# Weaving the routing, the metric of batch 0 and the first chunks into the projection loop of an adaLN block, with the layer normalisation moved from VectorE to GpSimd

## The reference, cut to what matters

```python
mod = (silu(c) @ wmod).reshape(8, 6, 1, 128)      # sa, ca, ga, sb, cb, gb
h = layernorm(x) * (1 + ca) + sa
x = x + ga' * attn(h)                              # ga', gb': sign(g) * max(|g|, 0.25)
h = layernorm(x) * (1 + cb) + sb
x = x + gb' * ffn(h)

# attn, 8 heads of 16, for each token t a causal window of 64 tokens
q, v = relu(h @ enc_q), relu(h @ enc_v)
sig  = q.mean(tokens) + 0.5 * q[::8].mean(tokens)              # one vector per batch
m    = softplus(base + 0.1 * (gelu(sig @ w1 + b1) @ w2 + b2))  # "metric", per batch
dist = sqrt(((q[window] - q[t])**2 * m).sum() + 1e-8)
keep the 32 nearest of the 64; w = exp(-dist) / sum
context = sum(w * v) + gate * 0.1 * (q / |q|) @ (U @ V)        # "Hebbian" term
attn = (q * context) @ decoder

# ffn: 8 experts of rank 64, mixed with gates that depend on token 0 of each batch
logits = h[:, 0] @ Wr.T ; gates = softmax over the two largest logits
ffn = h + sum_e gates[e] * (h @ A[e].T) @ B[e].T
```

## Time and profile before

| | us |
|---|---|
| three runs | 840.10, 841.48, 842.94 |
| the profiled execution | 845.14 |
| its span in the trace | 843.4 |
| first MAX8 of the first chunk | 91.19 |
| start of the fifth step of DVE (i = 4) | 140.29 |
| busy: DVE, PE, ACT, POOL | 788.9 (94% of the span), 718.6 (85%), 619.5 (73%), 463.0 (55%) |

### The profile page before, as it was taken

The page is one execution under the profiler, slowest core; times in us unless marked ns, Lnnn a source line. Parts: engine busy times, 40 slices in busy tenths (PEclk is TensorE's granted clock), DMA queues, the critical chain, the costliest instruction groups (busy, mean ns, idle before and its releaser), DMA issues.

```text
span 843.4 us, 21229 instructions
## 1 busy us (share of the span) xinstructions
PE 718.6 (85%) x4437; PEld 586.2 (70%) x4437; DVE 788.9 (94%) x6746; ACT 619.5 (73%) x1862; POOL 463.0 (55%) x871
## 2 busy tenths in 40 slices
PE   5997989888888888888888888888888888888845
PEld 3445677777777777777777777777777777777744
DVE  5855999999999999999999999999999999999980
ACT  3981368787777878777777877777878777787853
POOL 2112456666556566655656665565566655656541
PEclk9996989999999999999999999999999999999955
DMA  5310001101111110011110001111100111111000
GB/s 165 102 32 10 24 24 30 30 20 32 31 31 31 29 30 24 27 31 30 32 30 29 26 24 32 31 31 30 30 29 21 31 31 31 31 30 30 18 4 9
DMA packets 49232, 27.24 MB, mean 32 GB/s; under 512 B 5512, under 2 KB 48592, under 8 KB 49104
## 3 DMA queue, kind: packets, MB, share of 16 engines
q1 hardware_dynamic: 49104, 25.90, 10.4%
HBM read 10.28 MB, written 4.19 MB: 17 GB/s over the span
## 4 chain that ended last, share of the span: by engine, by line
DVE 83%; PE 10%; DMA 2%; ACT 2%; issue 2%; POOL 1%; SPq 1%; ACTq 0%; POOLq 0%
DVE work L976 44%; DVE m L965 29%; DVE key L998 4%; DMA big<-in_x 2%; DVE st_c L1007 1%; PE psD L1152 1%; DVE mv_c L1019 1%; PE psC L1182 1%; DVE key L787 1%; PE psD L1057 1%; DVE st_p L778 1%; PE psC L1085 1%; PE psW L1239 1%; DMA wmod_sb<-in_wmod 1%; PE psW L1168 1%
## 5 line engine op out<-in xcount | busy, mean ns | idle before, releaser
L976 DVE MATCH_REPLACE8 work<-m,work 128x64 f32<-128x64 f32 x1536 | 301.8, 208 | 0.0
L1152 PE MATMUL psD<-sst,tst 128*128 128x224 f32 x1024 | 238.9, 356 | 0.0
L965 DVE MAX8 m<-work 128x8 f32<-128x64 f32 x1536 | 209.9, 209 | 0.0
L1152 PEld LDWEIGHTS psD<-sst,tst 128*128 128x128 f32 x1024 | 196.3, 192 | 3.2 <-issue 0.3
L452 POOL TENSOR_TENSOR big<-work,con 128x512 f32<-128x512 f32 x128 | 162.2, 1291 | 13.0 <-ACT work L635 12.9
L481 POOL TENSOR_TENSOR t<-cst,qh 128x128 f32<-128x128 f32 x64 | 27.8, 434 | 232.3 <-ACT cst L714 232.3
L1182 PE MATMUL psC<-vst,big 128*128 128x34 f32 x1024 | 129.0, 272 | 0.0
L1182 PEld LDWEIGHTS psC<-vst,big 128*128 128x128 f32 x1024 | 128.4, 197 | 0.2
L976 DVE MATCH_VALUE_LOAD work<-m,work 128x8 f32 x1536 | 120.0, 78 | 0.0
L976 DVE MATCH_REPLACE8 work<-m,key 128x64 f32<-128x64 f32 x512 | 100.2, 208 | 0.0
L1149 PE MATMUL psD<-mask_bf,ident_bf 128*128 128x448 bf16 x256 | 91.1, 356 | 9.3 <-DMA tst<-nst 1.8
(11 more groups left out here) (199 smaller groups left out, 1474.7 us busy)
## 6 DMA issues: line engine op xcount, KB each, us to landing
hst<-hT_all SPq DMA_DIRECT2D x64, 96.0 KB
tst<-qT_all SPq DMA_DIRECT2D x256, 17.0 KB
big<-in_x SPq DMA_DIRECT2D x16, 256.0 KB, 2.8
tst<-nst SPq DMA_DIRECT2D x256, 1.0 KB
xs<-in_x SPq DMA_DIRECT2D x64, 64.0 KB, 1.9
out<-yo SPq DMA_DIRECT2D x64, 64.0 KB, 1.7
sst<-nst SPq DMA_DIRECT2D x128, 3.0 KB
con<-in_consts SPq DMA_DIRECT2D x1, 549.5 KB, 5.8
```

What stands on the lines that cost most here:

```text
L965: last = v.max(m8[:, h], src[:, h * WIN:(h + 1) * WIN])
L976: last = v.match_replace(work[:, s, cols], m8[:, h], src[:, cols], GONE)
L1152: last = mm(bank_of(r)[:, g, 0:SW], tst[:, s, r, g], sst[:, s, g], start=False, stop=(g == NG - 1), skip_group_check=True)
```

## The change: what it does

1. **Normalisation on POOL.** DVE only makes `nb = -mean * rstd` (one small instruction per unit, `nbias`), POOL does `x * rstd + nb` in four tensor_scalar instructions per unit. On ACT Ln and Exp of a unit now stand next to each other, between `to_hT(n+1)` and `to_q(n)`.
2. **Token 0 by itself.** Mean, variance, modulation and q of the eight first tokens are made ahead of unit 0 from `x0_sb` (`t0T`, `q0T`), so that the routing doesn't wait for the projection.
3. **`unit_extra(n)`.** On ACT, DVE and PE each unit n ends with a piece of the routing chain, of the metric of batch 0 (`METRIC[0]`), of the norms and values of chunks 0 and 1 (n = 10 to 13) and of the gate rows (n = 12 to 14).
4. **The other seven metrics** (`METRIC[1]`) run in steps 0 to 3 of the top-k: Gelu and its two table loads on ACT at i = 0, softplus on ACT at i = 1 and on POOL at i = 2 and 3, one reciprocal on DVE.
5. **Gate x B** is made wholly on POOL, in two halves of four 128x512 instructions; `experts(0)` is on PE at i = 0, `experts(1)` inside step 1, `expert_matrices(0)` on DVE inside step 0 and (1) ahead of step 2.
6. **Start of the pipeline.** `FIRST` is -1 instead of -3; the distances of chunk 0 follow the last unit on PE.
7. **Loads** are issued in another order; the constants are split so that the identity comes early; modn goes through psD instead of psW.

The core of the diff (SP's reordered issues, the pieces of `unit_extra` that only move, and the helper functions made of old lines are left out):

```diff
@@ POOL
+            def normalise(n):
+                u = n % 4
+                pool.wait_ge(nb_ready, n + 1)
+                need(pool, pT_ready, n - 1)
+                for c in range(4):
+                    last = nc.gpsimd.tensor_scalar(xn[:, u % 2, c], xp[:, u, c], rs_p[:, u, c:c + 1],
+                                                   nb_p[:, u, c:c + 1], ALU.mult, ALU.add)
+                last.then_inc(xn_ready, 1)
...
+            for n in range(5, NU):
+                normalise(n)
+                if n % 2:
+                    pads((n - 5) // 2)
...
+                if n in (12, 13):
+                    squares(n - 12)
+                    metric_of_norms(n - 12)
+                    metric_times_q(n - 12)
+            gates(0)
...
+            expert_rows(0)
+            pads(NB - 2)
+            gates(1)
+            expert_rows(1)
+            pads(NB - 1)
@@ ACT
+            def unit_extra(n):
+                if n == 0:
+                    act.wait_ge(pmod_ready, 2)
...                                                    # modn <- psD, two copies
+                if n == 3:
+                    act.wait_ge(r0_dve, 1)
...                                                    # Ln, Exp of the token norms
+                    gelu(0, psC)
+                if n == 4:
+                    exp_of_abs(0, psC)
+                if n == 6:
+                    act.wait_ge(r0_dve, 4)
...                                                    # Ln, Exp
+                if n in (10, 12):
+                    to_nst((n - 10) // 2)
+                if n in (11, 13):
+                    to_vst((n - 11) // 2)
+
+            for n in range(NU):
+                if n + 1 < NU:
+                    to_hT(n + 1)
+                if n + 3 < NU:
+                    invstd(n + 3)
+                to_q(n)
+                unit_extra(n)
...
+            for i in range(FIRST, LAST + 1):
+                if i == 0:
+                    gelu(1, psX)
+                if i == 1:
+                    exp_of_abs(1, psX)
...
+                step(i)
@@ DVE
+            def nbias(n):
+                u = n % 4
+                dve.wait_ge(rs_ready, n + 1)
+                need(dve, xn_ready, n - 3)
+                v.scalar_tensor_tensor(out=nb_p[:, u], in0=mv_p[:, u, :, 0], scalar=-1.0, in1=rs_p[:, u], op0=ALU.mult,
+                                       op1=ALU.mult).then_inc(nb_ready, 1)
...
+            for n in range(NU):
+                if n + 4 < NU:
+                    stats(n + 4)
+                if n + 3 < NU:
+                    nbias(n + 3)
+                unit_extra(n)
@@ PE
             def to_pT(n):
                 pe.wait_ge(xn_ready, n + 1)
                 need(pe, hT_ready, n - 1)
+                if n in (12, 14):
+                    pe.wait_ge(n2_ready, n // 2 - 5)
+                if n in (13, 15):
+                    pe.wait_ge(vst_ready, n // 2 - 5)
...
+            def unit_extra(n):
+                if n == 0:
...
+                    pe.wait_ge(modn_ready, 2)
...                                                    # Hebbian products, 4 pairs
+                if n == 4:
+                    metric_2(0, psC)
+                    pe.wait_ge(r0_dve, 2)
+                    nc.tensor.transpose(psX[:, 128:128 + NB], z8[:, 6], con[0:NB, 0:NB]).then_inc(r0_pe, 1)
...
+                if n == 7:
+                    pe.wait_ge(r0_dve, 5)
...
+                if n in (12, 13, 14):
+                    gate_rows(n - 12)
+
+            for n in range(NU):
+                if n + 1 < NU:
+                    to_pT(n + 1)
+                to_pq(n)
+                unit_extra(n)
...
+            distances(0, 0)
+            distances(0, 1)
+            pe.wait_ge(q_ready, 4 * NB)
+            distances(0, 2)
+            distances(0, 3).then_inc(dist_ready, 1)
+            gate_rows(3)
+
+            for i in range(FIRST, LAST + 1):
+                if i == 0:
+                    pe.wait_ge(gatew_ready, NB // 2)
+                    experts(0)
+                    metric_1(1, psX)
+                if i == 1:
+                    metric_2(1, psX)
+                step(i)
```

More of the change, by code:

```diff
@@ L314, in need, with there, metric, bsc @@
                 eng.wait_ge(s, value)
[L316 to L329, removed]
+        ROWS_IN = 16 * (NR + NG + NR)
+        FIRST, LAST = -1, NCH + 2
+        NU = 2 * NB
+        METRIC = (slice(0, 1), slice(1, NB))
+        def there(i, off, first=0):
+            return first <= i + off < NCH
         def column(k):
             return k * CH + (k // CPB) * WIN
+        def metric(j, part):
+            return sp[:, j].rearrange("p (g b) -> p g b", g=NG)[:, :, METRIC[part]]
+        def bsc(half, kt):
+            return big[:, kt // 2, half, (kt % 2) * 512:(kt % 2 + 1) * 512].rearrange("p (b d) -> p b d", b=4)
         block = ctx.enter_context(nc.Block())
@@ L361, in step @@
+            windows(0)
+            load(NU - 2)
+            load(NU - 1)
+            windows(1)
+            norms(0)
+            norms(1)
             def step(i):
@@ L370, in step @@
                     sync.dma_start(oc[:, k], yo[:, s]).then_inc(out_in[s], 16)
[L372 to L388, removed]
-            sync.wait_ge(pads_ready, 2 * NB)
-            sync.wait_ge(q_ready, 4 * NB)
-            sync.wait_ge(hT_ready, 2 * NB)
-            sync.wait_ge(ones_set, 7)
-            steps(step)
+                if there(i, 3, 2):
+                    windows(i + 3)
+                    norms(i + 3)
+            for i in range(FIRST, LAST + 1):
+                step(i)
             for s in range(2):
@@ L1028, in step @@
                 replaces(i, 3, 1)
-            steps(step, routing)
+            for i in range(FIRST, LAST + 1):
+                if i == 0:
+                    gate_weights(3)
+                if i == 2:
+                    expert_matrices(1)
+                if i == 3:
+                    dve.wait_ge(sp_pool, 2)
+                    v.reciprocal(metric(5, 1), metric(5, 1)).then_inc(sp_dve, 1)
+                step(i)
         @block.tensor
@@ L1219, in step @@
                     distances(s, 0)
[L1221 to L1227 removed]
+                if there(i, 2, 2):
+                    values(i + 2)
                 k, s = i + 2, (i + 2) % 2
```

774 lines of the change are left out of this document (434 added, 340 removed).

## The result

Measured: 861.37 us median (854.04 to 862.03) against 842.21 for the kernel before, ratio 1.021, 95% interval [1.015, 1.027]. A second measurement, of the same changed kernel beside the experiments, gave 856.48 (852.72 to 860.71) against 842.15, ratio 1.0173 [1.013, 1.0216]. Slower, which was the likeliest of the three outcomes forecast (0.45), but by 14 to 19 us where the forecast had 2.5; the range ended at 852.

What follows compares the result with a forecast made beforehand. DVE, busy 94% of the span, was taken as the bound, so only step 4's start counted: first pick -4.0, step 0 +5.45, steps 1 to 3 +1.0, sum +2.4, giving 844 us; range 831 to 852.

Steps and rivals of the forecast that it cites:

- q(15) at 80.4: End of ACT's last q of the projection, before at 57.93 us, forecast at 80.4; first pick then at 87.2.
- 11 + 3.2 for waits and clock: Projection: 11 us of waits between engines (bounds 0 and 14), 3.2 for PE's slower clock (bounds 0 and 9).
- Unit 6: Projection: ACT stalls 2.8 us for DVE's chain of 4.2 us, having only 1.4 of its own work.
- The start: Start of the projection, +1.8 us: unit 1's serial chain ends at 26.9 against 25.10 before.
- POOL's normalisation, 0: Projection: four instructions per unit on POOL at 0.30 us cost nothing; at 0.40 they cost +1.2 us.
- rival C: Projection: normalisation on POOL takes 0.46 us or more or slows DVE's statistics, +1.2 to +4, 847 us; chance 0.07.
- Step 0, +5.45: Top-k step 0: d2 of chunk 1 waits for expert products, metric product, Gelu and table load, adding 5.45 us.
- Steps 1 to 3, +1.0 with bounds 0 and 4: Top-k steps 1 to 3: PE falls to the low clock, distances(2) run late, d2 of step 1 waits 1 to 2 us.
- Nothing after step 4 moves except as a block: After 140.29 us: same instructions and tail, so only the start of step 4 matters.
- A: Projection slots work, answers ready when asked for: first pick at 73.0, 829.7 us, or 833.5 with part of the waits; chance 0.30.
- B: PE's clock stays low from unit 4 to 9, +8 less 3.2, and step 1 loses 2 more: 851 us; chance 0.18.
- D: Table loads on ACT: the skill's drain of 1.38 us per load holds, 848 us; chance 0.03.

Runs made afterwards that it cites:

- e1: Changed kernel with ACT's gelu(1) moved behind the key's Exp of chunk 1 in step 0; 67.3 us from first pick to step 5, against 79.4.
- e2: Changed kernel with ACT's four instructions on the second metric product behind chunk 0's squares in step 1; 70.3 us from first pick to step 5, against 79.4.
- e12: Changed kernel with POOL's six small metric instructions behind the two unfolds of step 3; steps 3 and 4 took 11.27 and 11.32 us, median 4.2 below 856.48.
- e3: Changed kernel plus 40 and 56 dummy bf16 products on PE ahead of steps 0 and 1, nothing reordered; 71.5 us from first pick to step 5, against 79.4.
- e7: e6 with the normalisation on DVE instead of POOL; median 839.17 us.
- e6: Changed kernel with the metric of batches 1 to 7 moved into idle places of PE, ACT, POOL and DVE; median 839.43 us.
- e8: e7 with DVE's metric reciprocal behind expert_matrices(0) and 11 and 20 dummy products ahead of chunk 1's distances and step 1; median 835.75 us.
- e9: e8 plus 22, 18 and 12 dummy fp32 products in PE's three longest waits of the projection (units 4, 7, 11); median 839.9 us.
- e10: Changed kernel plus only 22, 18 and 12 dummy fp32 products on PE in projection units 4, 7 and 11; executions took 855.61 to 857.89 us.

## Why the prediction was wrong, step by step

- **q(15) at 80.4: within its bounds, in part by luck.** 82.4 in the first profile, 76.6 to 77.8 in the six with an early first pick, 85.3 in the worst. ACT's waits from 24 us to q(15)'s end sum to 12.9 us in e1 and 17.4 in the changed kernel's first profile, against 11 + 3.2 for waits and clock. Unit 6 waited 2.29 (said: 2.8). The start was priced too long by 3 us: unit 1 ended near 24, not 26.9. The products of unit 0 took 2.25 us, not 3.78. "Slow clock" was also a misreading of the earlier trace rows: in the kernel before the granted clock is 1.00 all through those products, from 18.3 to 22.2, so why they took 3.78 stays open (from 36.79 in the first profile, at a mean of 0.53, such products took 3.57). That start, too late, and a clock that cost more in this profile than 3.2 partly cancel.
- **POOL's normalisation, 0: its rate was wrong.** 0.466 us an instruction against the 0.30 taken; it was outside the bounds of 0.30 and 0.40 and in rival C's territory (0.46 or more). By the early profiles it costs an estimated 1 to 2 us, which the medians don't confirm. The Trainium skill (GPSIMD Engine Reference, Engine selection) puts one-input forms near line rate; this form with two per-partition scalars took 1.35 times DVE's 344 ns. Its advice to stay on VectorE fits, its reason (two-input forms) was not the one at work.
- **Step 0, +5.45: measured +7.55.** The chain was named rightly and seen with `qh` as releaser: 7.43 us of wait. The 2 us missing are two banks of distances of chunk 1 at the low clock (0.50 and 0.66 at 88 to 92), which I priced at full speed.
- **Steps 1 to 3, +1.0 with bounds 0 and 4: measured +9.5 (second profile +8.8), and step 4 another +2.0 (second profile 0). This is the step that failed**, in three places. (a) `exp_of_abs(1)` ahead of the squares on ACT was not in the sum at all; it holds them from 109 to 112.6, and moving it alone gives 7.2 us back (e2). (b) "POOL's six small instructions at i = 3 about fill the slack": they cost 2.0 to 5.0 (e12), because the unfold behind them feeds PE. (c) "`experts(1)`, 3.6 us, fits into step 1": at the low clock it is 6.2 us and does not. The prediction saw that PE would fall to the low level and charged 1 to 2 us for the distances of chunk 2, but went on with durations of the high level for all behind them; a fall in one step lengthens the next step's PE work, which delays `qh` or the contexts, which makes DVE wait and lets PE idle again. e3 measures that loop: 6.0 us of the stretch, with no instruction moved.
- **Nothing after step 4 moves except as a block: nearly.** Steps from 5 on last 11.3 in both. From the first pick of the last chunk to the end it was 35.5 in the profile of before, 33.7 in the first and 35.5 in the second profile of the changed kernel, 32.2 in e3 and e7. Same instructions; by the windows the clock is at 0.50 from 805 to 843 in the kernel before and between 0.50 and 0.71 over the same part of e6 (32.1). So up to 3.5 us of a profile's time is scatter of the tail, which the sum took as fixed.
- **Rivals.** A (the slots work) is refuted: even in e1 ACT waited 12.9 us, where A would have had a third of 11 or nothing. The first picks of 83.4 to 84.6 owe most of their lead on 87.2 to the start, 2.9 us earlier than priced. C's rate held, and the estimate of 1 to 2 us lies at the low end of its 1.2 to 4, but POOL was not the pace maker: ahead of those 48 instructions it idled 19.2 us for DVE's `nb`. B named the right cause, the clock, in the wrong place: it put the loss in units 4 to 9, with only 2 us in step 1. D is refuted: behind the table load at 98.91 the relu began at 100.20, 0.01 us after its end. The upper bound of 4 for steps 1 to 3 should have come from the low level: the expert product alone is 2.65 more, and a set of four banks of distances 3.4 more (1.80 a bank from start to start instead of 0.94). With one product and two sets, 9.5, the range would have ended near 857, an estimate that takes in the second measurement and not the first.

## What to carry to other kernels

When a change puts a wait into a tuned pipeline, price the wait, then price everything that PE does after it at the low clock level, and then ask what waits for that: here a chain priced at 5 us stood at the head of a stretch that grew by 17 (the mean of 77.4 against 60.4). Read each queue from the moved instruction downwards: three of the moved pieces (a Gelu, four metric instructions, six small POOL instructions) stood ahead of work that DVE needed in that step, and moving them behind it, with nothing removed, took the stretch from 77.4 to 62.8 us. Where a gap of PE can't be closed, cheap dummy products sized to it kept the clock in e3 and e8; those of e9 cost 4.1 us against e8 of the same set.

## What the runs showed of the hardware

- The granted clock fell in different units in two executions of the same program: behind its first instruction the waits of PE over 0.3 us are the same up to 20 us (0.40 and 1.26, 0.39 and 1.26), and then the clock is 1.00 from 20 to 24 in one and 0.51 in the other. Over all profiles of the projection with the normalisation on POOL and without fillers the first pick lies between 83.4 and 92.1; the tail lies between 32.1 and 35.6 over all profiles. The Trainium skill (TensorE: Matmul & The Clock Gate, Part 1: The HAM clock gate) says that the number of slow matmuls of one kernel varies from run to run; the traces agree. It puts the penalty of the ramp at under 1% of a typical span. What e3 measures is wider than a ramp, since the waits that follow are in it: keeping PE busy in two gaps gave 6.0 us of the stretch, 0.7%. The medians, of two sets, differ by 9.9, 1.2%; e3's dummies stand behind the first pick, so the rest is scatter of the projection or lies in the tail.
- The clock also fell with no wait of PE in the trace: to 0.52 at 70 to 72 in e10, where PE is busy without a gap from 60 on.
- 20 bf16 products of 224 columns took 2.08 us at the high level (e8, 98.52), 0.10 each.
- A product of 8 matmuls of 512 columns, 3.60 to 3.70 us at the high level, took 6.18 (e6) to 6.25 us (first profile) where the level was low for most of it.
- An activation table load took 1.28 us, and the next instruction began 0.01 us after its end (98.91, then 100.20).
